# Sum of the attended values in a delta-rule decoder layer: the output halves of odd pairs are swapped and get a bank of their own

## The chip, the cores and the metric

One core of one Trainium2 chip. The time is device microseconds of one execution of the whole program, from the first to the last instruction with what the runtime counts around it; lower is better. Three runs of the kernel before gave a median of 2584.98 us (2584.34 to 2587.34).

TensorE (PE in the profile) multiplies. A product loads one operand into the array (LDWEIGHTS, engine PEld) and streams the other past it (MATMUL); the result lands in PSUM, eight banks of 128 partitions by 512 fp32. A product smaller than the array sits on a tile of it, `tile_position=(row, column)`: the rows are the partitions that the operands come from, the columns the partitions that the sum goes to. Products on different tiles can run at the same time. A product of fp32 operands is recorded as two LDWEIGHTS and two MATMULs. VectorE is DVE, ScalarE is ACT, GpSimd is POOL, and SyncE (SP) issues every DMA from one queue, in order. Engines wait for each other through semaphores.

## The reference

A decoder layer over 64 sequences of 64 tokens with 256 features: a gated delta-rule attention with 16 heads, then a cross attention, then a ternary feed-forward, each with its layer norm and its residual. Only the first part is touched. Cut to it:

```python
q = _causal_conv_silu(x @ Wq, qcw, qcb).reshape(b, t, HK, DK)
k = _causal_conv_silu(x @ Wk, kcw, kcb).reshape(b, t, HK, DK)
v = _causal_conv_silu(x @ Wv, vcw, vcb).reshape(b, t, HK, VE)
...
def step(state, inp):
    state = state * at
    err = vt - einsum('bhkv,bhk->bhv', state, kt)
    state = state + bt * einsum('bhk,bhv->bhkv', kt, err)
    return state, einsum('bhkv,bhk->bhv', state, qt)
...
out = outs.reshape(b, t, HV * DV) @ Wo
x = x + out
```

The kernel doesn't run the recurrence token by token. For each head it forms a 64x64 matrix M per sequence (the mix: how much of each earlier token's value goes to each token) and multiplies it with the values already multiplied by their part of Wo: `x + sum over heads of M_head @ (v_head @ Wo_head)`. That product with M is what the change rewrites.

## The kernel before, in words

**Tiling.** The 64 sequences are 8 groups (`G`) of 8. A group's 512 tokens are 4 pairs (`NP`, index `a`) of 128 partitions: partitions 0-63 hold one sequence of the pair (n = 0), 64-127 the other (n = 1). 8 groups by 16 heads are 128 heads, numbered through.

**The pipeline.** Each engine runs the same list of steps (`schedule`). A step has a value head `v` and a key head `k` that is 20 heads ahead; `w` is the head before `v`. 20 steps have only `k`, 108 have both, 20 have only `v`, and one more finishes the last head. The middle of the list is a hardware loop of 16 steps (`Fori`, run 6 times), with five jumps back between its rounds. Within a step, TensorE does in this order (function `step`, lines as in the profile):

1. `project(v,0)`, L1270: six 128x512 fp16 products into bank 0; it needs the `XV` tile (the group's normalized input, reloaded by DMA once a group, L355).
2. `values(w,0)`, L1284: twelve 128x256 products, into `VWB`; needs `low_values` of DVE (L1035).
3. `off_diagonal(v)`, L1305, needs two DMA loads (`ld_pv` L388, `ld_en` L377); `query_sums(k-2)`, L1312, needs the squares that POOL makes (L626); `diagonal(v)`, L1321.
4. `project(v,1)`, `values(w,1)`, `correction(v)` (L1334), `project(k,2)`.
5. `outputs(w)`, **L1348**: the mix of values, eight products M (64x64) times VW (64x256), both fp32, added up over the 16 heads of a group in the banks `AC[0]` and `AC[1]`. It needs the values as ACT has scaled them (L788) and M from DVE (L1030).
6. `grams(k-1)`, L1364, and `project(k,3)`.

ACT makes the first convolution tap (`tap`, L762), the silus (L768, L769, L776) and the scaling of the values (L788). DVE adds the other three taps of each of the four convolutions (L1020), makes M, the low parts of the values (L1035) and the decayed key products (L1043), which SP stores to memory (`spill`, L395).

**Every eighth step** a batch of heads goes through POOL, which inverts 32x32 triangles lane by lane (L587 to L621). For it SP has in its queue, behind the store of that step: `store_lanes` (three DMAs), `load_beta` (four), the loads for the next value head (`load_values`: up to eleven), and a step later `load_lanes` (four, L415). POOL's squares for `query_sums` come behind the first operations of the batch in POOL's order.

**Once a group** (every 16 steps): SP loads the group's rows of x into `XP[:,0]` (`residual` of SP, L447, in the step with v mod 16 = 2), DVE adds the two banks to it (`residual` of DVE, L1052, v mod 16 = 1), and SP stores the sum to `X1D` (`keep`, L452, same step). The first `outputs` of the next group waits for DVE's two adds. After the last group, the second part of the kernel (cross attention and feed-forward) starts by reading `X1D` back (`rows`, L538).

The present order of tiles in `outputs`: for each pair `a`, n = 0 on tile (0,0) and n = 1 on tile (64,64), into bank `AC[a // 2]`, columns `256 * (a % 2)`. Only two tiles of 64x64 are ever used.

The second part of the kernel has a product whose tiles are 32 rows by 64 columns (`scores`, L1437), eight of fp32 with 256 streamed columns each:

```python
for c in range(2):
    for n in range(2):
        for j in range(2):
            r = 2 * h + j
            ins = mm(SCB[h][j][64 * n:64 * n + 64, 256 * c:256 * c + 256], QT[...], KG[...],
                     start=True, stop=True, tile_position=(32 * r, 64 * n))
```

Its four tiles are two groups of rows times two groups of columns, and each group of rows writes a bank of its own (j).

Of the kernel before, what the change touches and what calls it, by code (L numbers as in the profile page):

```python
# [6 lines left out]
ALU = mybir.AluOpType  # L7
# [4 lines left out]
ds = bass.ds  # L12
# [3 lines left out]
E = 256  # L16
NB = 64
GT = 512
G = NB * T // GT
NP = GT // P  # L20
NH = 16
# [39 lines left out]
def build(nc, x, ctxT, ctxR, wall, wo, wab, cw, w1, b1, w2, b2, cst, out):  # L61
    ctx = ExitStack()
    with ctx:
        def sb(name, shape, dt=F32):
            return ctx.enter_context(nc.sbuf_tensor(name, shape, dt))

        def sem(name):
            return ctx.enter_context(nc.semaphore(name))
# [15 lines left out]
        XP = sb("XP", [P, 2, NP, E])  # L84
# [18 lines left out]
        M = sb("M", [P, 2, NP, T])  # L103
# [13 lines left out]
        def dram(name, shape, dt=F32):  # L117
            return nc.dram_tensor(name, shape, dt).ap()
# [10 lines left out]
        X1D = dram("X1D", [G, P, NP, E])  # L129
# [7 lines left out]
        VW = XN[:, 1]  # L137
# [49 lines left out]
        AC = BANK[6:8]  # L187
# [22 lines left out]
        S = {n: sem(n) for n in names}  # L210
# [7 lines left out]
        def at(count):  # L218

            return count + 1  # L220


        def heads(h, per=1, more=0):

            g, off = h
            return g * (NH * per) + (off * per + more + 1)
# [16 lines left out]
        def groups(h, per=1, more=0):  # L243

            g, off = h
            return g * per + ((off // NH) * per + more + 1)
# [43 lines left out]
        def _(sp):  # L290
# [12 lines left out]
            for g in range(G):  # L303
# [9 lines left out]
                if g >= 4:  # L313
                    n = g - 4
# [119 lines left out]
            def store_lanes(k):  # L434
# [5 lines left out]
                sp.dma_start(KND[b].rearrange("o p x -> (o p) x"), KNL[:, :]).then_inc(S["st_le"], 16)  # L440
                sp.dma_start(QND[b].rearrange("o p x -> (o p) x"), QNL[:, :]).then_inc(S["st_le"], 16)

            def residual(g):

                sp.wait_ge(S["st_x1"], at(g * 16))
                sp.nop(nofuse=True)
                sp.dma_start(XP[:, 0], x[ds(g, 1)].rearrange("o p n e -> (o p) n e")).then_inc(S["ld_xa"], 16)  # L447

            def keep(g):
                sp.wait_ge(S["xa_done"], at(g * 2 + 2))  # L450
                sp.nop(nofuse=True)
                sp.dma_start(X1D[ds(g, 1)].rearrange("o p n e -> (o p) n e"), XP[:, 0]).then_inc(S["st_x1"], 16)  # L452

            def stored_eq(units):
                for s in range(2):
# [9 lines left out]
            def step(v, k):  # L465
# [13 lines left out]
                if exists(v):  # L479
                    v1 = (v[0], v[1] + 1)  # L480
                    if exists(v1):
                        load_values(v1)
                        if v1[1] % NH == 0:
                            load_xv(v1)
                    if v[1] % NH == 1 and after(v, NH):
                        keep(v[0] + (v[1] // NH - 1))
                    if v[1] % NH == 2:
                        residual(v[0] + v[1] // NH)
# [39 lines left out]
            def attended(i):  # L528
                s = i % 2
                if i >= 2:  # L530
                    sp.wait_ge(S["vb_done"], at(2 * i - 2))
                for n in range(2):
                    sp.dma_start(VTS[s][64 * n:64 * n + 64], ctxR[i]).then_inc(S[f"ld_vt{s}"], 16)

            def rows(i):
                s = i % 3
                sp.wait_ge(S[f"st_out{s}"], at(16 * (i // 3)))
                sp.dma_start(XC[s], X1D[i]).then_inc(S[f"ld_y{s}"], 16)  # L538
# [5 lines left out]

            keys(0)
            keep(G - 1)
            attended(0)
            sp.wait_ge(S["st_x1"], at(16 * G))
            rows(0)
            rows(1)  # L550
            keys(1)
# [343 lines left out]
        def _(dve):  # L895
            start_counts(dve, "dve")
            V_ = nc.vector
# [148 lines left out]
            def residual(g):  # L1046

                dve.wait_ge(S["out_mm"], at(g * NH + NH))
                dve.wait_ge(S["ld_xa"], at(g * 16 + 16))
                for n in range(2):  # L1050
                    xv = XP[:, 0, 2 * n:2 * n + 2, :].rearrange("p a e -> p (a e)")
                    V_.tensor_tensor(xv, AC[n][:, :], xv, ALU.add).then_inc(S["xa_done"], 1)  # L1052

            def step(v, k):
                if exists(v):
                    if v[1] % NH == 1 and after(v, NH):
                        residual(v[0] + (v[1] // NH - 1))
# [29 lines left out]

            schedule(dve, step)
            residual(G - 1)

            def arrived(i):
# [119 lines left out]
        def _(pe):  # L1211
            start_counts(pe, "pe")
            mm = nc.tensor.matmul
# [124 lines left out]
            def outputs(w):  # L1338
                g, off = w
                pe.wait_ge(S["vw_ev"], heads(w, 2, 2))  # L1340
                pe.wait_ge(S["m_done"], heads(w, 1, 1))
                if off % NH == 0:
                    pe.wait_ge(S["xa_done"], groups(w, 2))
                pe.nop(nofuse=True)
                for a in range(NP):
                    for n in range(2):
                        b = slice(64 * n, 64 * n + 64)
                        ins = mm(AC[a // 2][b, E * (a % 2):E * (a % 2) + E], M[b, off % 2, a, :], VW[b, a, :],  # L1348
                                 start=(off % NH == 0 and a % 2 == 0), stop=(off % NH == NH - 1), tile_position=(64 * n, 64 * n), skip_group_check=True)
                ins.then_inc(S["out_mm"], 1)  # L1350

            def grams(v, k):
# [14 lines left out]
            def step(v, k):  # L1367
# [24 lines left out]
                if exists(w):  # L1392
                    outputs(w)
# [195 lines left out]
```

## Time and profile before

| | |
|---|---|
| median of three runs | 2584.98 us |
| the profiled execution: its own time | 2580.95 us |
| span in its profile | 2579.1 us |
| granted TensorE clock, mean over the span | 0.933 |
| busy: PE, DVE, ACT, POOL | 86%, 71%, 57%, 42% |
| L1348, the mix of values | 2048 records, 248.9 us busy, 7% of the chain that ended last |
| the 128 blocks of L1348 | first at 357.1 us, last record starts at 2018.0 us |

How to read it: the profile was taken of one execution, whose own time is 4.0 us below the median of the three; the span leaves 1.9 us of that time outside. Busy time of an engine counts overlapping records once. "Idle before" an operation, with an arrow, names what the engine waited for; "issue" is a wait for nothing that the profile shows.

### The profile page before, as it was taken

The numbers are of one execution on the slowest core, as the hardware profiler recorded it, in microseconds if no ns is written. First come the engines' busy times: TensorE is split into PE (matmuls) and PEld (weight loads), VectorE is DVE, ScalarE is ACT, GpSimd is POOL, SyncE is SP. The second block draws the span as 40 slices with busy tenths as digits, with TensorE's granted clock in tenths as the row PEclk, the third lists the DMA queues.
The fourth block names the chain that finished last, engine by engine and source line by source line (L and its number), as shares of the span: only waits on it lengthen the run. The fifth ranks groups of instructions, "written<-read, shape, count | busy, mean of one in ns | idle before, by whom it ended". The sixth has DMA issues, their size and how long they took to land.

```text
span 2579.1 us, 64198 instructions
## 1 busy us (share of the span) xinstructions
PE 2218.8 (86%) x22592; PEld 1422.6 (55%) x22592; DVE 1841.7 (71%) x2925; ACT 1477.5 (57%) x2755; POOL 1088.6 (42%) x1439
## 2 busy tenths in 40 slices
PE   2486689999999999999999999999888688778787
PEld 2232245656655565565555556566555466666665
DVE  7775577877878887787778878878555545655655
ACT  3475556666666666666666666666555344544544
POOL 1016484572845638356283653836620111212222
PEclk9998889999999999999999999999999658878878
DMA  7446523243242333324324233342421101100100
GB/s 292 143 116 134 132 73 83 78 97 85 71 99 79 83 90 88 87 68 92 95 68 95 88 79 84 96 89 63 97 57 39 53 13 30 30 27 29 29 14 18
DMA packets 500783, 205.23 MB, mean 80 GB/s; under 512 B 437072, under 2 KB 454224, under 8 KB 498512
## 3 DMA queue, kind: packets, MB, share of 16 engines
q1 hardware_dynamic: 500432, 200.76, 30.7%
q8 instruction: 195, 3.19, 0.5%
q14 instruction: 156, 1.28, 0.2%
HBM read 128.33 MB, written 72.35 MB: 78 GB/s over the span
## 4 chain that ended last, share of the span: by engine, by line
PE 56%; issue 13%; SPq 8%; ACT 8%; DVE 8%; DMA 4%; POOL 2%; ACTq 0%; POOLq 0%; DVEq 0%
PE PS L1270 16%; PE PS L1284 10%; PE PS L1348 7%; PE PS L1456 3%; PE PS L1437 3%; PE PS L1470 3%; PE PS L1364 3%; DVE Y L1020 3%; ACT XN L788 3%; PE PS L1321 2%; PE PS L1498 2%; ACT Y L769 2%; SPq L377 1%; DMA SCR<-PGD 1%; SPq L431 1%
## 5 line engine op out<-in xcount | busy, mean ns | idle before, releaser
L1020 DVE SCALAR_TENSOR_TENSOR Y<-PS,CW,Y 128x504 f32<-128x504 f32 (+2 forms) x1536 | 1115.3, 732 | 442.5 <-ACT Y L762 389.9
L762 ACT ACTIVATE Y<-PS,CW 128x512 f32<-128x512 f32 x512 | 398.1, 777 | 466.4 <-PE PS L1270 454.8
L1284 PE MATMUL PS<-WOS,XN 128*128 128x256 f16 x3072 | 378.2, 273 | 2.2 <-DVE XN L1035 1.1
L1284 PEld LDWEIGHTS PS<-WOS,XN 128*128 128x128 f16 x3072 | 300.9, 98 | 92.9 <-issue 2.1
L626 POOL TENSOR_TENSOR SQ<-KQ 128x512 f32<-128x512 f32 x128 | 137.6, 1075 | 461.8 <-PE PS L1312 370.3
L1270 PE MATMUL PS<-XK,WH 128*128 128x512 f16 x1024 | 312.6, 387 | 16.3 <-DMA XK<-XHD 16.3
L1270 PE MATMUL PS<-XV,WH 128*128 128x512 f16 x1024 | 307.5, 382 | 8.4 <-issue 7.8
L612 POOL TENSOR_TENSOR SCR<-SCR 128x31 f32<-128x31 f32 (+15 forms) x496 | 291.2, 587 | 38.9
L1348 PE MATMUL PS<-XN,M 64*64 64x256 f32 x2048 | 248.9, 381 | 48.9 <-ACT XN L788 48.0
L609 POOL TENSOR_TENSOR SCR<-SCR 128x31 f32<-128x31 f32 (+15 forms) x496 | 260.3, 525 | 33.0
L788 ACT ACTIVATE XN<-PS,KN 128x256 f32<-128x256 f32 x512 | 212.6, 466 | 62.6 <-PE PS L1284 62.5
L1348 PEld LDWEIGHTS PS<-XN,M 64*64 64x64 f32 x2048 | 158.3, 132 | 137.6 <-issue 101.5
L768 ACT ACTIVATE XN<-Y 128x512 f16<-128x512 f32 x256 | 160.1, 626 | 77.2 <-PE PS L1284 74.5
L1270 PE MATMUL PS<-XK,WL 128*128 128x512 f16 x512 | 197.0, 385 | 0.0
L1035 DVE TENSOR_TENSOR XN<-Y,XN 128x512 f16<-128x512 f32 x256 | 186.6, 729 | 12.0 <-ACT Y L769 12.0
L1270 PE MATMUL PS<-XV,WL 128*128 128x512 f16 x512 | 194.7, 380 | 0.0
L776 ACT ACTIVATE KQ<-Y 128x512 f32<-128x512 f32 x256 | 159.8, 625 | 41.2 <-DVE Y L1020 27.8
L865 ACT ACTIVATE WH<-PS 128x512 f32<-128x512 f32 x128 | 73.6, 596 | 176.3 <-PE PS L1456 176.3
L769 ACT ACTIVATE Y<-Y 128x512 f32<-128x512 f32 x256 | 157.5, 615 | 0.0
L692 POOL CAST WH<-WOS 128x512 f16<-128x512 f32 x64 | 40.1, 627 | 274.9 <-ACT WOS L874 273.4
L1364 PE MATMUL PS<-KQ 128*64 128x128 f32 x2048 | 140.9, 280 | 11.4 <-ACT SCR L802 10.2
L1270 PEld LDWEIGHTS PS<-XV,WH 128*128 128x128 f16 x1024 | 87.6, 98 | 112.5 <-issue 20.3
(138 smaller groups left out, 3152.3 us busy)
## 6 DMA issues: line engine op xcount, KB each, us to landing
PGD<-SCR SPq DMA_DIRECT2D x128, 256.0 KB, 2.1
SCR<-PGD SPq DMA_DIRECT2D x128, 256.0 KB, 3.1
EQD<-XN SPq DMA_DIRECT2D x32, 512.0 KB, 4.1
SCR<-EQD SPq DMA_DIRECT2D x128, 128.0 KB, 2.6
SCR<-QND SPq DMA_DIRECT2D x128, 128.0 KB, 3.3
XP<-in_x SPq DMA_DIRECT2D x16, 512.0 KB, 4.6
SCR<-in_wall SPq DMA_DIRECT2D x8, 1024.0 KB, 7.1
SCR<-PGD SPq DMA_DIRECT2D x64, 128.0 KB, 3.0
```

The costliest lines, as they stand in the source:

```text
L609: nc.gpsimd.tensor_tensor(t, LP[:, j, j + 1:BL][:, :, None].broadcast_to([P, n, m]), LY[:, j, 0:m][:, None, :].broadcast_to([P, n, m]), AL ...
L612: nc.gpsimd.tensor_tensor(LY[:, j + 1:BL, 0:m], LY[:, j + 1:BL, 0:m], t, ALU.subtract).then_inc(S["lane"], 1)
L762: A_.activation(Y[:, b, :], PJ[b][:, :], ACT.Identity, scale=CW[:, h[1] % NH, cw0 + 3:cw0 + 4], bias=CW[:, h[1] % NH, cw0 + 4:cw0 + 5]).th ...
L768: A_.activation(VHL[:, 0, b, :], Y[:, b, :], ACT.Silu)
L769: A_.activation(Y[:, b, :], Y[:, b, :], ACT.Silu).then_inc(S[f"silu{b}"], 1)
L788: ins = A_.activation(VW[:, a, :], VWB[:, E * i:E * i + E], ACT.Copy, scale=KN[:, kn, l:l + 1])
L1020: V_.scalar_tensor_tensor(yv[:, :, m:T], pv[:, :, 0:T - m], CW[:, h[1] % NH, cw0 + 3 - m:cw0 + 4 - m], yv[:, :, m:T], ALU.mult, ALU.add).t ...
L1035: V_.tensor_tensor(VHL[:, 1, b, :], Y[:, b, :], VHL[:, 0, b, :], ALU.subtract).then_inc(S["vl_done"], 1)
L1270: ins = mm(PJ[b][:, :], wt[:, c, w0:w0 + P], xb[:, xi, :], start=(n == 0), stop=(n == 5))
L1284: ins = mm(VWB[:, E * i:E * i + E], VHL[:, vk, n, P * a:P * a + P], WOS[:, wk, 2 * (w[1] % NH) + n, :], start=(t == 0), stop=(t == 5))
L1348: ins = mm(AC[a // 2][b, E * (a % 2):E * (a % 2) + E], M[b, off % 2, a, :], VW[b, a, :], start=(off % NH == 0 and a % 2 == 0), stop=(off % ...
L1364: ins = mm(gram[64 * n:64 * n + 64, a], KQ[:, s, 0, c0:c0 + 64], KQ[:, s, :, c0:c0 + 64], start=True, stop=True)
```

## The change

`outputs` gives the products of odd pairs the swapped column half: output tile (64n, 64((n + a) mod 2)). The even pairs go to bank `AC[0]` (tiles (0,0) and (64,64)), the odd pairs to `AC[1]` (tiles (0,64) and (64,0)); so the sums of odd pairs lie with the two sequences in swapped halves of the partitions. `residual` of DVE therefore adds bank n to the pairs n, n+2 (a strided view), and the rows of x are loaded and stored with the odd pairs' halves swapped: three DMAs in place of one, for the load and for the store, and the counts of `ld_xa` and `st_x1` go from 16 to 48 a group.

```diff
+            def swapped(sums, rows):
+
+                yield sums[:, 0:NP:2, :], rows[:, 0:NP:2, :]
+                yield sums[0:64, 1:NP:2, :], rows[64:128, 1:NP:2, :]
+                yield sums[64:128, 1:NP:2, :], rows[0:64, 1:NP:2, :]
+
             def residual(g):
 
-                sp.wait_ge(S["st_x1"], at(g * 16))
+                sp.wait_ge(S["st_x1"], at(g * 48))
                 sp.nop(nofuse=True)
-                sp.dma_start(XP[:, 0], x[ds(g, 1)].rearrange("o p n e -> (o p) n e")).then_inc(S["ld_xa"], 16)
+                xg = x[ds(g, 1)].rearrange("o p n e -> (o p) n e")
+                for dst, src in swapped(XP[:, 0], xg):
+                    sp.dma_start(dst, src).then_inc(S["ld_xa"], 16)
 
             def keep(g):
                 sp.wait_ge(S["xa_done"], at(g * 2 + 2))
                 sp.nop(nofuse=True)
-                sp.dma_start(X1D[ds(g, 1)].rearrange("o p n e -> (o p) n e"), XP[:, 0]).then_inc(S["st_x1"], 16)
+                x1 = X1D[ds(g, 1)].rearrange("o p n e -> (o p) n e")
+                for src, dst in swapped(XP[:, 0], x1):
+                    sp.dma_start(dst, src).then_inc(S["st_x1"], 16)
...
-            sp.wait_ge(S["st_x1"], at(16 * G))
+            sp.wait_ge(S["st_x1"], at(48 * G))
...
                 dve.wait_ge(S["out_mm"], at(g * NH + NH))
-                dve.wait_ge(S["ld_xa"], at(g * 16 + 16))
+                dve.wait_ge(S["ld_xa"], at(g * 48 + 48))
                 for n in range(2):
-                    xv = XP[:, 0, 2 * n:2 * n + 2, :].rearrange("p a e -> p (a e)")
-                    V_.tensor_tensor(xv, AC[n][:, :], xv, ALU.add).then_inc(S["xa_done"], 1)
+                    xv = XP[:, 0, n:NP:2, :]
+                    V_.tensor_tensor(xv, AC[n][:, :].rearrange("p (a e) -> p a e", e=E), xv, ALU.add).then_inc(S["xa_done"], 1)
...
-                if off % NH == 0:
+                first = off % NH == 0
+                if first:
                     pe.wait_ge(S["xa_done"], groups(w, 2))
                 pe.nop(nofuse=True)
                 for a in range(NP):
                     for n in range(2):
-                        b = slice(64 * n, 64 * n + 64)
-                        ins = mm(AC[a // 2][b, E * (a % 2):E * (a % 2) + E], M[b, off % 2, a, :], VW[b, a, :],
-                                 start=(off % NH == 0 and a % 2 == 0), stop=(off % NH == NH - 1), tile_position=(64 * n, 64 * n), skip_group_check=True)
+                        b, o = slice(64 * n, 64 * n + 64), 64 * ((n + a) % 2)
+                        ins = mm(AC[a % 2][o:o + 64, E * (a // 2):E * (a // 2) + E], M[b, off % 2, a, :], VW[b, a, :],
+                                 start=(first and a < 2), stop=(off % NH == NH - 1), tile_position=(64 * n, o), skip_group_check=True)
```

## Rows read from the trace of the kernel before

**Rows 1.** The profile page: its head, busy times, and one of its costliest groups.

```profile
span 2579.1 us, 64198 instructions
...
PE 2218.8 (86%) x22592; PEld 1422.6 (55%) x22592; DVE 1841.7 (71%) x2925; ACT 1477.5 (57%) x2755; POOL 1088.6 (42%) x1439
...
L1348 PE MATMUL PS<-XN,M 64*64 64x256 f32 x2048 | 248.9, 381 | 48.9 <-ACT XN L788 48.0
```

**Rows 2.** Two stretches: length, busy by engine, PEclk, DMA share, GB/s.

```profile
1021.58:1034.72 13.14, 12.99 (x136) 8.04 (x137) 11.12 (x18) 8.69 (x18) 6.56 (x3) 1.00 0.23 57
...
1061.00:1075.32 14.32, 13.07 (x137) 8.09 (x137) 10.76 (x17) 8.64 (x18) 2.51 (x3) 1.00 0.65 131
```

**Rows 3.** Waits of PE, 360 to 2000 us: total us, times, longest.

```profile
...
PE PS L1312 <- POOL SQ L626: 15.8, 13, 1.9
PE PS L1305 <- DMA SCR<-PGD: 12.4, 12, 1.6
PE PS L1270 <- issue: 7.8, 5, 1.7
PE PS L1305 <- issue: 2.2, 1, 2.2
```

**Rows 4.** Timeline of PE in one step: start, length, line, records, idle before.

```profile
1021.58 1.94 PE L1348 MATMUL PS<-XN,M 64*64 64x256 f32 x16 [0.15 <-ACT XN L788]
1023.45 1.09 PE L1364 MATMUL PS<-KQ 128*64 128x128 f32 x16
```

**Rows 5.** The same view in the second part: L1437, fp32, 256 columns.

```profile
2200.53 1.09 PE L1437 MATMUL PS<-SCR,KQ 32*64 32x256 f32 x16
```

**Rows 6.** Timeline of DVE in the same step as rows 4.

```profile
1025.24 0.68 DVE L1043 TENSOR_TENSOR SCR<-PS,SCR 128x512 f32<-128x512 f32 x1
1026.80 4.46 DVE L1020 SCALAR_TENSOR_TENSOR Y<-PS,CW,Y 128x504 f32<-128x504 f32 x6 [0.88 <-ACT Y L762]
```

**Rows 7.** Timeline of SP's queue, 1050 to 1084 us.

```profile
1052.26 0.36 SPq L395 DMA_DIRECT2D PGD<-SCR  x1
...
1065.68 0.36 SPq L388 DMA_DIRECT2D SCR<-PGD  x1
```

**Rows 8.** Timeline of PE over the same stretch.

```profile
1047.86 1.94 PE L1348 MATMUL PS<-XN,M 64*64 64x256 f32 x16 [0.15 <-ACT XN L788]
...
1069.08 0.44 PE L1305 MATMUL PS<-SCR 32*32 32x32 f32 x16 [1.10 <-DMA SCR<-PGD]
...
1083.57 0.43 PE L1312 MATMUL PS<-SQ,ONES 128*32 128x128 f32 x8 [0.91 <-POOL SQ L626]
```

**Rows 9.** Timeline of POOL, 1070 to 1084 us.

```profile
1072.81 0.32 POOL L587 TENSOR_SCALAR KD<-SCR 128x32 f32<-128x32 f32 x1 [16.03 <-DMA SCR<-PGD]
...
1082.38 1.04 POOL L626 TENSOR_TENSOR SQ<-KQ 128x512 f32<-128x512 f32 x1
```

**Rows 10.** Timeline of ACT in the step behind the loop's jump.

```profile
1019.56 0.63 ACT L768 ACTIVATE XN<-Y 128x512 f16<-128x512 f32 x1 [0.30 <-DVE Y L1020]
```

**Rows 11.** The XV load: SP's issue, its landing (view of L355), PE's next projection.

```profile
979.93 0.35 SPq L355 DMA_DIRECT2D XV<-XHD  x1
...
DMA to landing us min/median/max: 3.9/4.2/4.8
...
984.42 0.59 PE L1270 MATMUL PS<-XV,WH 128*128 128x512 f16 x2
```

**Rows 12.** Timeline of DVE and PE, last steps.

```profile
1904.84 1.94 PE L1348 MATMUL PS<-XN,M 64*64 64x256 f32 x16 [1.55 <-ACT XN L788]
...
1905.96 0.69 DVE L1035 TENSOR_TENSOR XN<-Y,XN 128x512 f16<-128x512 f32 x1 [0.62 <-ACT Y L769]
...
1908.02 1.47 PE L1284 MATMUL PS<-WOS,XN 128*128 128x256 f16 x12
```

**Rows 13.** Timeline of SP's queue where it stores a group's rows (L452).

```profile
1004.90 0.38 SPq L452 DMA_DIRECT2D X1D<-XP  x1
1010.91 0.34 SPq L395 DMA_DIRECT2D PGD<-SCR  x1
```

## The prediction

> **What bounds the kernel now.** I read the page first: PE is busy 86% of a span of 2579.1 us, and the block that the change rewrites has 2048 records, 16 for each of 128 heads [rows 1]. Then the busy time by stretches: in a plain step of 13.14 us PE is busy 12.99 at full clock, DVE 11.12, ACT 8.69 [rows 2]. So TensorE sets the pace, and the reader should see how near DVE is: 2.0 us of slack in 13.14. Then PE's waits [rows 3]: 13 for POOL's squares, 12 for a DMA and one more listed as issue (2.2), 5 at the loop's jumps; before the mix of values itself it waits for ACT, 0.15 us in a plain step [rows 4] and 1.55 in the last steps [rows 12]. The waits of rows 3 decide how much of a gain survives.
>
> **The price of the block.** From the start of the mix to the start of the next block PE spends 1023.45 - 1021.58 = 1.87 us, and its 16 records span 1.94 [rows 4]. One record of fp32 with 256 columns, if pairs share the array, has 1.87 / 8 = 0.23 us a pair. The block of scores has the same number of records, columns and type, on four tiles (two groups of rows by two of columns), and spans 1.09 [rows 5]. That is the shape that the change asks for, so the block should shrink by 1.94 - 1.09 = **0.85 us**. Bounds: nothing at all if the four don't overlap; not more than half of 1.87, 0.94. I take 0.85, from the nearest row. What rows 5 don't show: tiles of 64 rows instead of 32, and two groups of rows in one bank (each keeps to its own half of the partitions, as the pairs of rows 4 do today).
>
> The page TensorEngine Tiling (Array Packing) of the Trainium skill, section Gotcha 1: PSUM Pressure, says that different row tiles cannot use the same PSUM bank at the same time. Today tiles (0,0) and (64,64) are two row tiles in one bank, and they do overlap: alone, 16 records of a pair's 0.23 us would take 3.7 us, not 1.94. By that rule the change could give nothing; it is rival B.
>
> **Plain steps.** The wait before the mix (0.15) hangs on ACT, which hangs on PE's own `values` product before it; between the two lie `correction` and a projection, which don't change. So the wait stays and the 0.85 passes on to `grams` and `project(k,3)`. What is late next? DVE: it finishes L1043 at 1025.24 + 0.68 = 1025.92 and then idles 0.88 us for the tap of that projection [rows 6]. The tap comes 0.85 sooner and 0.03 of idle is left. It just fits; the squeezed step is 12.29 us with 11.12 of DVE in it. A plain step gives the full 0.85.
>
> **Steps around a POOL batch.** Here a chain runs beside PE. SP waits for DVE's L1043, stores at 1052.26, and then issues without a break (three stores, four loads of beta, six for the next values) until the load of L388 at 1065.68 [rows 7]; PE waits for that at 1069.08, 1.10 us [rows 8]. The lanes' load goes out behind it; POOL starts on it at 1072.81 and comes to the squares 9.57 us later, at 1082.38 [rows 9]; PE waits for them until 1083.57 [rows 8]. The chain starts 4.4 us behind the mix of 1047.86, after DVE work that the change doesn't touch. It is SP's, the DMA's and POOL's time from there on, so 1083.57 stays 35.7 us behind 1047.86 whatever PE saves between. Three mixes lie in it (at 1047.86, 1061.00 and 1075.32; the stretch between the latter two stands in [rows 2]). Their 0.85 turn into longer waits: 1.10 becomes 2.8, 0.91 becomes 1.8. With 13 such batches [rows 3] that takes 39 blocks. The last batch has only the first wait (the one listed as issue): 2 more. 128 - 41 = 87 blocks count: 87 x 0.85 = 74.0 us.
>
> **The loop's jumps.** Behind a jump ACT starts L768 at 1019.56 with 0.30 us of waiting for DVE, not PE [rows 10]; DVE has lost its own time to the jump. PE's next mix hangs on it, so the block before each of the five jumps gives nothing either (I take 0.8 lost of 0.85): -4.0 us.
>
> **The XV load.** SP issues it at 979.93, behind the same kind of burst; it lands 4.2 us later, at about 984.13, and PE starts on it at 984.42 [rows 11]. PE would now come at 983.57 and wait some 0.6, with the landing's spread (up to 4.8) 0.7. Of the seven loads I count five so tight: -3.5 us.
>
> **The last 20 steps.** PE idles 1.55 us a step for ACT, behind its own `values`, so the mix is still on the path. DVE's low part is done at 1905.96 + 0.69 = 1906.65 and `values` starts at 1908.02 [rows 12]: 1.37 of slack for 0.85. Full gain, already in the 87.
>
> **DMAs and DVE's adds.** Load and store of the group's rows go from 1 DMA to 3, +4 issues a group, at the store's 0.38 us and with 0.2 between two issues some 2.3 us on SP. They come in steps with v mod 16 = 1 and 2, the bursts with v mod 8 = 4 and 5. What is queued behind them is the next `spill`, which waits for DVE: behind the store, issued at 1004.90, it goes out at 1010.91, with 5.6 us of nothing between [rows 13]. That gap hides the new issues. If it were gone: 8 x 2.3 = 18 us. Only the very last store is in the open, since the second part reads it back: 2 more issues, +0.7 us (bounds: 0 and 3, should the smaller pieces land a microsecond later each). DVE's two adds keep their element count: 0; bounds -0.2 and +0.3 us a group, on DVE, whose slack takes it.
>
> **Sum:** 74.0 - 4.0 - 3.5 - 0.7 = 65.8 us less. The profiled execution took 2580.95; 2580.95 - 65.8 = 2515. The median of the three runs is 4.0 above that execution, so the forecast for it is **2519 us**, 2.5% less.
>
> **Rivals.**
> - **A2, nothing absorbed.** If the chains at the batches move along with PE, up to 128 x 0.85 = 109 us: 2476. Against it: SP's issues and POOL's 9.57 us have fixed lengths. The middle (half of the 41 blocks saved) is 2500. Chance 0.08 for anything below 2498.
> - **B, two at a time still.** A bank serves one group of rows (or the halves of a 64-row tile block each other): no gain, and the DMAs: 2585 to 2588. For it: rows 5 keep one bank to each group of rows, as if someone had to. Against it: today's pairs share a bank. Chance 0.06.
> - **C, DVE takes over.** Its idle of 0.88 is used up to 0.03. If in the plain steps the taps slip by half the gain, 0.42 x 87 = 37 us are lost: 2556. For it: DVE at 11.12 of 12.29 us, and its two adds in one step of 16. Against it: DVE has begun L1043, and so is done with the low parts, at 1025.24 [rows 6], while PE has `grams` (begun at 1023.45, rows 4) and two projections before it asks for them. Chance 0.10 for 2548 and more.
> - **E, slower.** The array must run empty at each turn between the diagonal and the crossed pairs: three turns a block. A turn costs up to one pair's time, 0.23; the point of decision is any price over zero with no overlap of the four. Half of it: 3 x 0.12 x 128 = 45 us, 2630; whole: 2675. Against it: rows 5 turn in the same way, and 1.09 leaves no room for it. Chance 0.03.
> - The change does as it says: the four tiles of one round are (0,0), (64,64), (0,64), (64,0), all different.
>
> **How the numbers follow.** My forecast's own range is 2498 to 2540 (blocks at 0.75 to 0.94, 80 to 107 of them counting, DMA terms at their ends), chance 0.73. The range is 2498 to 2550, which reaches to the near end of C and leaves out A2, B, E and the rest of C. A measurement tells about 0.2% (5 us) from no change. Faster by more: A, A2, C, 0.91; within: B, 0.05; slower: E and a bad end of B, 0.04.
>
> **What would show it.** L1348: 16 records in 1.09 us, starts in fours. Plain step 12.3 us; the last steps 0.85 shorter too. PE's waits for POOL and for `PGD` loads up from 15.8 and 12.4 to some 27 and 34; about five for `XV`. DVE's idle of 0.88 gone. I would be wrong in the price if L1348 stays at 1.94 or lands between; wrong in the bound if the block is 1.09 and the plain step isn't 12.3; wrong on the batches if their waits don't grow.

## The result, and the profile after

The changed kernel takes 2552.34 us (2548.81 to 2560.02, four runs), the kernel before 2586.16 us (2584.34 to 2588.78); ratio 0.9873, interval 0.9859 to 0.9886. It is faster by 1.3%, 34 us. The forecast was 2519, with a range up to 2550: the sign was right, the size half of what was forecast, and the time lies just outside the range.

The profile page of the changed kernel: its head, the busy times, and two of its costliest groups. The lines of the code have moved down by 10 or 11.

```profile
span 2547.2 us, 64266 instructions
...
PE 2140.5 (84%) x22592; PEld 1352.7 (53%) x22592; DVE 1854.4 (73%) x2925; ACT 1476.6 (58%) x2755; POOL 1086.6 (43%) x1439
...
L1280 PE MATMUL PS<-XV,WH 128*128 128x512 f16 x1024 | 318.9, 394 | 21.3 <-DMA XV<-XHD 10.7
...
L1359 PE MATMUL PS<-XN,M 64*64 64x256 f32 x2048 | 140.1, 387 | 51.0 <-ACT XN L798 47.9
```

TensorE's 2048 records of the mix (L1359, before L1348) now cover 140.1 us where they covered 248.9 [rows 1]: 108.8 us less. In the trace the records of a block now start in fours (0, 8, 14 and 21 ns into it, the next four from 239 ns on), where before they started in pairs (0 and 7, then 238): the four tiles do run at a time. The timeline of TensorE over a batch, the counterpart of [rows 4, 8]:

```profile
1040.91 1.09 PE L1359 MATMUL PS<-XN,M 64*64 64x256 f32 x16 [0.15 <-ACT XN L798]
1041.94 1.09 PE L1375 MATMUL PS<-KQ 128*64 128x128 f32 x16
...
1053.20 1.09 PE L1359 MATMUL PS<-XN,M 64*64 64x256 f32 x16
...
1063.01 0.64 PE L1315 MATMUL PS<-SCR 32*32 32x32 f32 x16 [3.68 <-DMA SCR<-PGD]
...
1071.77 1.09 PE L1359 MATMUL PS<-XN,M 64*64 64x256 f32 x16 [0.15 <-ACT XN L798]
...
1078.32 0.43 PE L1322 MATMUL PS<-SQ,ONES 128*32 128x128 f32 x8
...
1084.19 1.09 PE L1359 MATMUL PS<-XN,M 64*64 64x256 f32 x16
```

The block spans 1.09 us (1.94 in rows 4), and the plain step 1053.20 - 1040.91 = 12.29 us, as forecast. Then comes the load's wait: 3.68 us where it was 1.10. The forecast had 2.8 for it, so 0.9 us is lost against the forecast up to its end. More is lost behind it: from the load's release to the next mix TensorE needs 1071.77 - 1063.01 = 8.76 us; before it needed 1075.32 - 1069.08 = 6.24 for the same products (the time of the mix at 1075.32 is the end of the second stretch of [rows 2]). Why is in the view by stretches (length, busy time by engine, then PEclk, DMA share, GB/s):

```profile
1042.00:1048.00 6.00, 6.00 (x76) 3.84 (x76) 5.66 (x9) 3.61 (x8) 0.06 (x1) 1.00 0.21 69
1062.76:1066.00 3.24, 2.99 (x42) 1.95 (x43) 0.00 (x0) 0.68 (x3) 0.00 (x0) 0.50 1.14 204
1066.00:1070.00 4.00, 4.00 (x32) 2.33 (x31) 1.16 (x2) 1.07 (x3) 2.75 (x3) 0.67 0.25 74
```

Before the wait the granted clock is 1.00 (2.4 GHz); when TensorE comes out of it, it is 0.50 (1.2 GHz), and 0.67 on the mean over the next 4 us. The page TensorE: Matmul & The Clock Gate of the Trainium skill, in Part 1 (the clock gate), lists these two levels and lets idle lead to the lower; the trace agrees here, with 0.50 behind 3.68 us of idle (further down stands a wait of nearly that length that left 1.00). In the kernel before, 1.10 us of idle left the clock at 1.00. Over the whole stretch from the first mix to the last the clock records of the trace hold two stretches at half clock, 6.8 us together, before the change, and 18, 75.1 us together, after it: 12 at the batches, two behind waits for XV (the tile of the group's input), one behind a jump and three in the last 20 steps.

The other waits of TensorE in the changed kernel (total us, times, longest), to be held against [rows 3]:

```profile
PE PS L1315 <- DMA SCR<-PGD: 37.6, 14, 4.2
PE PS L1322 <- POOL SQ L636: 17.5, 11, 3.4
PE PS L1280 <- DMA XV<-XHD: 10.7, 4, 3.4
PE PS L1280 <- issue: 10.6, 5, 2.8
```

The load's waits went from 12.4 to 37.6 us (forecast: 34), the squares' from 15.8 to 17.5 (forecast: 27), and XV waits appeared: 10.7 us over 4. One of those, in three views: SP's issue, TensorE's start, and the stretch behind it (length, busy by engine, PEclk, DMA share, GB/s):

```profile
755.79 0.35 SPq L355 DMA_DIRECT2D XV<-XHD  x1
```

```profile
760.22 0.60 PE L1280 MATMUL PS<-XV,WH 128*128 128x512 f16 x2 [3.41 <-DMA XV<-XHD]
```

```profile
760.22:764.40 4.18, 4.18 (x22) 2.36 (x24) 1.58 (x3) 0.78 (x1) 3.71 (x7) 0.64 0.26 75
```

It waits 3.41 us, and the clock behind it is 0.64 again.

**Where the time went.** From the starts of the 128 mixes: a plain step fell from 13.14 to 12.29, which over the 107 steps from the first mix to the 108th would be 91.0 us. What these steps take beyond a plain one rose from 42.3 to 111.5 us, so 69.2 of the 91.0 were given back. In parts:

| excess over plain steps, us | before | after | rise | forecast |
|---|---|---|---|---|
| 13 batches, three steps each | 32.0 | 78.3 | 46.3 | 33.2 |
| steps with the XV load (6) | 0.8 | 14.7 | 13.9 | 3.5 |
| steps behind the five jumps | 8.9 | 15.9 | 7.0 | 4.0 |

The first row is 13 times the mean length of the three steps of a batch (41.88 before, 42.89 after) less three plain ones (39.42 and 36.87). The three rows make 67.2 of the 69.2. Most of the other 2 us stands in four steps that are 0.39 us longer; in each TensorE waits 0.22 us for DVE's low parts (L1045). The 20 steps from the 108th mix to the last fell from 210.9 to 200.4 us, and from the last mix on the kernel takes 564.4 us instead of 562.7.

### The profile page after: what moved, and what is told of

Its sections match the earlier page's. It is cut to its first block, busy times and chain, and to the rows that moved or that the text cites. A ratio compares the mean times of both kernels' runs of the same rounds, so it can differ in the third digit from the quotient of the medians.

```text
span 2547.2 us, 64266 instructions
## 1 busy us (share of the span) xinstructions
PE 2140.5 (84%) x22592; PEld 1352.7 (53%) x22592; DVE 1854.4 (73%) x2925; ACT 1476.6 (58%) x2755; POOL 1086.6 (43%) x1439
## 4 chain that ended last, share of the span: by engine, by line
PE 50%; issue 13%; DVE 13%; SPq 10%; ACT 8%; DMA 5%; POOL 1%; ACTq 0%; DVEq 0%; POOLq 0%
PE PS L1280 15%; PE PS L1294 9%; DVE Y L1030 5%; PE PS L1467 3%; PE PS L1448 3%; PE PS L1481 3%; PE PS L1359 3%; PE PS L1375 2%; PE PS L1509 2%; PE PS L1331 2%; ACT XN L798 2%; SPq L377 2%; DMA SCR<-PGD 2%; SPq L431 2%; ACT Y L779 2%
## 5 line engine op out<-in xcount | busy, mean ns | idle before, releaser
L1294 PE MATMUL PS<-WOS,XN 128*128 128x256 f16 x3072 | 386.9, 277 | 3.7 <-DVE XN L1045 2.7
L1294 PEld LDWEIGHTS PS<-WOS,XN 128*128 128x128 f16 x3072 | 305.4, 100 | 104.1 <-issue 9.9
L1280 PE MATMUL PS<-XV,WH 128*128 128x512 f16 x1024 | 318.9, 394 | 21.3 <-DMA XV<-XHD 10.7
L1045 DVE TENSOR_TENSOR XN<-Y,XN 128x512 f16<-128x512 f32 x256 | 199.7, 780 | 12.2 <-ACT Y L779 12.2
L1280 PE MATMUL PS<-XV,WL 128*128 128x512 f16 x512 | 201.6, 394 | 0.0
L1359 PE MATMUL PS<-XN,M 64*64 64x256 f32 x2048 | 140.1, 387 | 51.0 <-ACT XN L798 47.9
L1375 PEld LDWEIGHTS PS<-KQ 128*64 128x64 f32 x2048 | 109.8, 137 | 67.0 <-issue 45.5
```

The source lines that it names most:

```text
L1045: V_.tensor_tensor(VHL[:, 1, b, :], Y[:, b, :], VHL[:, 0, b, :], ALU.subtract).then_inc(S["vl_done"], 1)
L1280: ins = mm(PJ[b][:, :], wt[:, c, w0:w0 + P], xb[:, xi, :], start=(n == 0), stop=(n == 5))
L1294: ins = mm(VWB[:, E * i:E * i + E], VHL[:, vk, n, P * a:P * a + P], WOS[:, wk, 2 * (w[1] % NH) + n, :], start=(t == 0), stop=(t == 5))
L1359: ins = mm(AC[a % 2][o:o + 64, E * (a // 2):E * (a // 2) + E], M[b, off % 2, a, :], VW[b, a, :], start=(first and a < 2), stop=(off % NH = ...
L1375: ins = mm(gram[64 * n:64 * n + 64, a], KQ[:, s, 0, c0:c0 + 64], KQ[:, s, :, c0:c0 + 64], start=True, stop=True)
```

## The experiments

Twelve kernels ran, four at a time beside the kernel before. A median of the kernel before holds for the kernels named behind it until the next one is given.

### Fill the idle of the first wait

```diff
+                if v[1] % 8 == 6:
+                    for _ in range(12):
+                        mm(CH[:, :], IDH[:, :], MASKN[:, :, :].rearrange("p h t -> p (h t)"), start=True, stop=True)
                 pe.wait_ge(S[f"ld_pv{s}"], pairs(v, 16, 16))
```

> The changed kernel with 12 throw-away products (fp16, 512 columns, 0.216 us each at full clock, 2.6 us in all) on TensorE ahead of the wait for the L388 load, in the one step of eight where that wait is long (37.6 us over 14 waits in the changed kernel). They go to a bank that holds nothing at that moment. Theory 1 (the idle of about 3 us drops TensorE's clock to half for 3.4 to 6.8 us, and that is what was lost): the clock drops around the batches vanish (19 stretches between 340 and 1970 us in the changed kernel, most behind such a wait), the time falls by 10 to 25 us, to 2527 to 2542, although TensorE does 34 us of work more. Theory 2 (SP's queue and the DMA landings alone set the loss, the clock is a bystander): the waits shrink by what the fillers take, the time stays within 3 us of 2552 or rises.

2546.66 us (before 2583.25; ratio 0.9864, interval 0.9841 to 0.9888). The half-clock stretches behind the load's wait went, but 17 stretches, 58.0 us together, stood elsewhere: ten behind the wait for the squares, four behind the jumps, three in the last steps. The waits for the squares and for the load:

```profile
PE PS L1325 <- POOL SQ L636: 30.0, 13, 2.7
PE PS L1318 <- DMA SCR<-PGD: 2.3, 3, 1.0
```

The load's wait fell to 2.3 us, that for the squares rose from 17.5 to 30.0. So TensorE came sooner to the second wait, as its end is set by POOL, and lost its clock there in ten of the 13 batches. The three steps of a batch took 43.3 us on the mean, not less than the 42.9 of the changed kernel. Neither theory was right by itself; the ratio can't be told from 0.9873.

### Shorten the chain: seven DMAs a step earlier

```diff
-                if ph == 0 and exists(back(k, 16)):
-                    store_lanes(back(k, 16))
-                if ph == 0 and exists(back(k, 8)):
-                    load_beta(back(k, 8))
+                if ph == 7 and exists(back(k, 15)):
+                    store_lanes(back(k, 15))
+                if ph == 7 and exists(back(k, 7)):
+                    load_beta(back(k, 7))
```

In the changed kernel:

> The changed kernel, with store_lanes and load_beta (seven DMAs, some 5.2 us of SP's issue time) moved from the step where the next value head's loads wait behind them to the step before. Both theories say that the chain of SP, DMA and POOL ends 5 us sooner, so the waits for the PGD loads (37.6 us) and for POOL's squares (17.5 us) go to nearly nothing, and with them the clock drops behind them: 2586 - 128 x 0.85 - 28 (the waits of the kernel before) + 8 for jumps and XV loads = about 2457; range 2440 to 2480. If the blocks' gain were lost to something else than this chain (DVE, say), it would stay above 2500.

2503.9 us (ratio 0.9698, interval 0.9666 to 0.9729): 48 us below the changed kernel, but 47 above what I expected, and above the 2500 that I had set as the sign of another cause. In the kernel before:

> The same move of store_lanes and load_beta in the kernel before, without the change. Its waits at the batches are 28.2 us (15.8 for POOL, 12.4 for the DMA), and there are nearly no clock drops (6.8 us of half clock): so 2586 - 28 = 2558, range 2550 to 2565. Together with the run of the same move on the changed kernel it tells what the change is worth when the chain is not in its way: theory: 128 x 0.85 = 109 us less a few for the loop's jumps, 95 to 109.

2557.48 us (ratio 0.9901, interval 0.9878 to 0.9924), as expected. The waits for the squares, first of the changed kernel with the move, then of the kernel before with it, and the timeline of TensorE around one such wait in the first of them, with the stretch behind it:

```profile
PE PS L1322 <- POOL SQ L636: 33.3, 13, 3.4
```

```profile
PE PS L1312 <- POOL SQ L626: 11.2, 13, 1.1
```

```profile
410.65 1.09 PE L1359 MATMUL PS<-XN,M 64*64 64x256 f32 x16 [0.15 <-ACT XN L798]
...
419.90 0.65 PE L1322 MATMUL PS<-SQ,ONES 128*32 128x128 f32 x8 [2.76 <-POOL SQ L636]
...
427.24 1.09 PE L1359 MATMUL PS<-XN,M 64*64 64x256 f32 x16 [0.15 <-ACT XN L798]
```

```profile
420.00:423.60 3.60, 3.60 (x30) 1.82 (x31) 0.00 (x0) 0.72 (x3) 2.94 (x9) 0.55 0.57 39
```

The load's wait is gone in both. The squares' wait is not: it has 11.2 us in the kernel before, 33.3 in the changed one, over 13 each. What I had overlooked is that the chain is not one but two: the move frees the load of L388, while the lanes' load still waits for the step's store, and POOL still makes its first operations (9.57 us, rows 9) before the squares. The faster TensorE comes to that wait 3 x 0.85 us sooner; the wait grew by 1.7 us on the mean, since the squares too were ready a little sooner (34.16 us behind the batch's first mix, 34.50 in the kernel before with the move). Behind the wait shown the clock is 0.55. From the squares' release to the next mix it takes 427.24 - 419.90 = 7.34 us there; in every batch without such a stretch it is 5.87, in this kernel, in the changed one and in the kernel before alike. **A half-clock stretch with nothing behind it that waits longer costs about 1.5 us** (with one, the way from release to mix takes 7.2 to 7.6 us in all these kernels). The kernel before with the move has no such stretch from its first mix to its last.

Not every wait of this length is followed by one. The longest wait for the squares in the changed kernel with the move is 3.43 us, and the clock stays at 1.00 in it and behind it (timeline of TensorE, then the stretches of the wait and behind it):

```profile
841.37 0.43 PE L1322 MATMUL PS<-SQ,ONES 128*32 128x128 f32 x8 [3.43 <-POOL SQ L636]
```

```profile
837.90:841.38 3.48, 0.05 (x5) 0.04 (x3) 2.31 (x4) 1.07 (x3) 3.32 (x5) 1.00 0.56 28
841.38:845.00 3.62, 3.62 (x42) 2.37 (x42) 0.34 (x1) 1.50 (x4) 2.92 (x10) 1.00 0.47 51
```

Nine of the 13 waits for the squares in this kernel have a half-clock stretch behind them, four have not; what decides is not shown.

### The squares ahead of POOL's first operations

```diff
+                if ph == 2 and exists(back(k, 1)):
+                    squares(back(k, 1))
                 if exists(kb):
                     if ph == 2:
                         lanes_begin(kb)
...
-                if exists(back(k, 1)):
+                if ph != 2 and exists(back(k, 1)):
                     squares(back(k, 1))
```

With the seven DMAs moved as well. In the changed kernel, and then in the kernel before:

> The changed kernel with two moves: the seven DMAs of store_lanes and load_beta a step earlier, as before, and in POOL's batch step the squares ahead of lanes_begin instead of behind its 9.6 us. What is left of batch waits with the first move alone is 33.3 us for POOL's squares over 13 waits, and 14 half-clock stretches (48 us up to 1930 us) behind them. Theory (fixed chains and the clock behind their waits took the gain): both go, 33 us of waits and up to 24 us of clock: 2504 - 33 - 20 = 2451, range 2440 to 2465. Rival (DVE, or SP at the XV load, takes the gain): above 2480.

> The same two moves in the kernel before. With the first move alone its waits for the squares are 11.2 us and it has no half-clock stretch between 350 and 1950 us: 2557 - 11 = 2546, range 2540 to 2552. The difference to the changed kernel with both moves is what the four tiles are worth when nothing else is in their way; theory 90 to 105 us (128 x 0.85 less the loop's jumps and the split DMAs).

2485.42 us (before 2588.07; ratio 0.9595, interval 0.9565 to 0.9625) and 2553.59 us (ratio 0.9867, interval 0.984 to 0.9894). No wait for squares is left in either. The first lies in the rival's range (above 2480), not in the theory's, and the rival had named the XV load: the next chain had come up. The second is 1.6 us above its range. The difference of the two kernels is 68 us, not the 90 to 105 expected. TensorE's largest new wait in the changed kernel with both moves, and the same in the kernel before with both:

```profile
PE PS L1282 <- DMA XV<-XHD: 22.7, 7, 4.3
```

```profile
PE PS L1272 <- DMA XV<-XHD: 10.9, 6, 2.4
```

### Fill the idle, once more

Twelve products of 512 columns ahead of the load's wait and 14 of 384 columns ahead of the squares', in the changed kernel; and the 14 alone, in the changed kernel with the seven DMAs moved:

```diff
             def query_sums(k):
+                if k[1] % 8 == 1:
+                    for _ in range(14):
+                        mm(CH[:, 128:512], IDH[:, :], MASKN[:, 0:6, :].rearrange("p h t -> p (h t)"), start=True, stop=True)
                 pe.wait_ge(S["sq"], heads(k, 1, 1))
```

> The changed kernel with throw-away products ahead of both waits of a batch: 12 of 512 columns before the L388 load's, 14 of 384 columns before POOL's squares (2.3 us). The chain of SP and POOL is as in the changed kernel; only TensorE's idle is filled. With the first fill alone, 16 half-clock stretches were left (55 us, most of them behind the wait for the squares) and the time was 2547. Theory 1 (the clock takes a part of the loss): stretches fall to below 6, the time to 2547 - 16 = 2530, range 2522 to 2540. Theory 2 (the clock is a bystander, since the waits' ends are set by SP and POOL): 2545 to 2550.

> The changed kernel with the seven DMAs moved, and 14 throw-away products of 384 columns ahead of the wait for POOL's squares, which stays (33 us over 13 in the run without the fill). Theory 1: the 14 half-clock stretches (48 us) go, each worth 1.7 us: 2504 - 20 = 2484, range 2478 to 2490. Theory 2: 2500 to 2506.

2548.82 us (ratio 0.9847, interval 0.9814 to 0.9879) and 2505.46 us (ratio 0.9686, interval 0.9657 to 0.9715). The clock came back as meant: 5 stretches (23.9 us) and 3 (13.7 us) were left, and from release to mix the first kernel takes 5.87 us in all 13 batches, the second in 12 of them (7.45 in the first batch). The time did not follow: both lie in the ranges of theory 2. The fill in the second kernel:

```profile
1051.62 2.45 PE L1321 MATMUL PS<-MASKN,IDH 128*128 128x384 f16 x14
...
1055.49 0.42 PE L1325 MATMUL PS<-SQ,ONES 128*32 128x128 f32 x8 [1.42 <-POOL SQ L636]
...
1061.35 1.09 PE L1362 MATMUL PS<-XN,M 64*64 64x256 f32 x16 [0.15 <-ACT XN L798]
```

It lies within the wait (1.42 us are left), so it is not the fill itself. Two things took the gain back. The squares' release came later behind the batch's first mix: 34.67 us on the mean, 34.16 without the fill (and 37.01 with both fills, 36.53 in the changed kernel). The last of the four loads of lanes took 3.70 us to land here, 2.82 without the fill; why is open. So of the 0.9 us a batch that the clock gave back (6.90 us from release to mix became 5.99), 0.4 was left, some 5 us in all. And the steps behind the five jumps took 24.2 us over plain ones here, 26.0 in the kernel with both fills, against 13.7 to 19.3 in the seven kernels with the four tiles that have no fill or only the one ahead of the load's wait. In three of the five, TensorE waits a second time in both kernels with the 14 products (L1294, 0.7 to 1.5 us, "issue"), which happens in none of the others. More instructions stood in the loop's body. That these made the jumps dearer is my reading, not tested by itself. What the runs show is that filling the idle raises the clock and gains nothing that can be measured here, while removing the wait does.

### The XV load sooner, and the split DMAs

```diff
-                        load_values(v1)
-                        if v1[1] % NH == 0:
-                            load_xv(v1)
+                        load_values(v1, (lambda: load_xv(v1)) if v1[1] % NH == 0 else None)
```

where `load_values` now calls what it is given behind its EN loads. With the two moves before, in the changed kernel and in the kernel before:

> The changed kernel with the two moves for the batches and a third: the XV load goes to SP's queue in the middle of the next head's loads (behind the four of EN, ahead of T1 and PGV) instead of behind them all. With two moves TensorE waits 22.7 us over 7 times for XV. The load goes out some 2 us sooner, so each wait (3.2 us on the mean) shrinks to about 1.2 and the half-clock stretches behind them (10 left) mostly go: 2485 - 14 - 10 = 2461, range 2452 to 2472. If the wait is not set by SP's queue but by the projection that frees the tile, nothing changes: 2480 to 2488.

> The same three moves in the kernel before. Its waits for XV with two moves were 10.9 us over 6; they should go: 2553 - 9 = 2544, range 2538 to 2550. Against the changed kernel with the same moves it gives what the four tiles are worth with the chains out of the way: theory 128 x 0.85 = 109 less 8 for the loop's jumps and 9 for the split DMAs: 80 to 95 us.

2455.52 us (before 2583.59; ratio 0.9506, interval 0.9478 to 0.9533) and 2539.4 us (ratio 0.9832, interval 0.9806 to 0.9857). Both in their ranges. TensorE's waits behind the jumps (issue) and for XV in the first, and behind the jumps in the second, which has none for XV:

```profile
PE PS L1282 <- issue: 11.5, 5, 2.5
PE PS L1282 <- DMA XV<-XHD: 3.1, 6, 0.9
```

```profile
PE PS L1272 <- issue: 7.9, 5, 1.8
```

The difference of the two kernels is the worth of the change with these chains out of the way: 2539.4 - 2455.5 = 84 us, against 34 with them (54 with the first move in both, 68 with two).

The split DMAs were looked at from both ends: alone in the kernel before, and taken out of the changed kernel (the sequences of odd pairs swapped on the host, so that load and store are one DMA again and the second part works on swapped pairs), without and with the three moves.

```diff
-                for dst, src in swapped(XP[:, 0], xg):
-                    sp.dma_start(dst, src).then_inc(S["ld_xa"], 16)
+                sp.dma_start(XP[:, 0], xs[ds(g, 1)].rearrange("o p n e -> (o p) n e")).then_inc(S["ld_xa"], 16)
...
+    xs = a["x"][perm].reshape(G, NP, P, E).transpose(0, 2, 1, 3)
+    c = a["ctx_512"][perm]
```

> The kernel before with only the DMAs of the change: load and store of a group's rows in three pieces each, halves not swapped, two tiles as before. In the changed kernel the way from the last add to the second part's first LayerNorm product grew: TensorE waits 14.98 us there against 13.09. Theory: 1.5 to 2.5 us slower than before, all of it at the end of the first part, the group's loads and stores in the loop cost nothing. Rival: the splits also disturb the loop (more packets, SP later at the XV load): 5 us and more.

> The change as it is, only without the split DMAs (sequences of odd pairs swapped on the host instead). If the 9.6 us that the split cost the kernel before are a cost of the change too: 2552 - 9 = 2543, range 2539 to 2547. If it is hidden behind the longer waits of the changed kernel apart from the end of the first part: 2549 to 2552.

> The changed kernel with the three moves and without the split DMAs: the sequences of odd pairs are swapped on the host (a second, permuted copy of x for the residual, permuted context, permuted rows of the result), so load and store of a group's rows are one DMA each again and the second part works on swapped pairs. The split alone cost the kernel before 9.6 us (2592.8 against 2583.3). Theory: 5 to 10 us less than with the three moves and the split: about 2454, range 2445 to 2462.

Alone in the kernel before: 2592.81 us against 2583.25 (ratio 1.0037, interval 1.0023 to 1.0052), so 9.6 us slower and not 2. Of that, 1.7 us stand at the end of the first part; the waits for its first norm and for the squares are

```profile
PE PS L1426 <- DVE XN L1116: 14.8, 1, 14.8
PE PS L1322 <- POOL SQ L636: 19.8, 13, 2.6
```

(13.1 us in the kernel before; the squares' wait was 15.8.) In its profile four batches have a half-clock stretch behind the squares, where the kernel before has one, and their way from release to mix is 7.5 us. The two profiled executions lie 15.6 us apart: the three steps of a batch took 42.54 us on the mean, 41.88 before, which is 8.6 us over the 13, and from the last mix on it is 568.8 us against 562.7. Taken out of the changed kernel, the split gives nothing: 2552.35 us (before 2583.59; ratio 0.9871, interval 0.9839 to 0.9903). In that kernel's profile the batches took 8.5 us less and the steps with the XV load 12.5 more than in the changed one: what one chain gave, the other took. Taken out where the waits are gone, the kernel takes 2449.64 us (ratio 0.9485, interval 0.946 to 0.951) against 2455.52; the intervals of the two ratios overlap, so the 6 us are likely but not shown. That kernel is the best of the study, 5.2% below the kernel before.

## Why the prediction was wrong

The step that failed is the price of the waits around TensorE. The prediction let a wait grow by the blocks saved, 33.2 us at the batches and 3.5 at the XV loads, and put what stands behind it at nothing. Measured were 46.3 and 13.9 us: the clock behind the waits, a chain that itself ended later, and XV waits that grew beyond the saved block.

**The price of the block held.** 1.09 us as in rows 5, 0.85 saved, in all 128 heads. Rivals B and E are out: two row tiles in one bank, each on its own half of the partitions, and crossed with two others in a second bank, overlap at the rate of the scores' block. The rule of the Trainium skill on row tiles and banks (TensorEngine Tiling (Array Packing), Gotcha 1: PSUM Pressure) does not hold in the form quoted in the prediction: both traces are against it. Two row tiles that write the same partitions of one bank were not tried.

**Plain steps held**, 12.29 us to the hundredth; so did the last ones (9.62 for 10.47). Rival C is out: DVE kept up, but for the four steps of 0.39 us more. It idles 0.20 us before the tap of `project(k,3)`, where 0.03 was left by my sum:

```profile
1045.28 4.45 DVE L1030 SCALAR_TENSOR_TENSOR Y<-PS,CW,Y 128x504 f32<-128x504 f32 x6 [0.20 <-ACT Y L772]
```

**Steps around a batch: the mechanism was right, a term was missing.** "1083.57 stays 35.7 us behind 1047.86 whatever PE saves between": over the 13 batches the squares' release stood 35.88 us on the mean behind the batch's first mix before, and 36.53 after. Three savings a batch were absorbed, as forecast, and the runs with shortened chains show that it is this chain (34 us of gain with it, 84 without it and the XV chain). Two things came on top. The chain itself grew by 0.65 us. On the mean it didn't grow up to the load of L388, whose release stood 21.08 us behind the first mix before and 21.09 after, but behind it: the last of the four loads of lanes landed 0.42 us later (25.37 for 24.95), POOL's first operations took 9.70 us for 9.57, and in the first batch TensorE itself came 0.8 us late to the squares, at half clock. Single batches also lose ahead of L388: in the one above, four EN loads took 4.43 us (SP's timeline, issue to issue):

```profile
1045.31 0.36 SPq L395 DMA_DIRECT2D PGD<-SCR  x1
...
1053.01 4.43 SPq L377 DMA_DIRECT2D SCR<-ED  x4
...
1059.53 0.36 SPq L388 DMA_DIRECT2D SCR<-PGD  x1
...
1061.55 2.96 SPq L415 DMA_DIRECT2D SCR<-PGD  x4
```

From the first to the L388 load it is 14.22 us, where rows 7 have 13.42. What slows the issues and the landings wasn't found. And a wait of TensorE was booked at its length alone. It has a second price, the clock behind it. Behind the first wait of a batch the second wait mostly hides that (in 8 of the 12 batches with such a stretch the way from release to mix was the plain 5.87 us); behind the second it does not. Together 1.0 us a batch (0.65 the chain, 0.4 the clock behind the second wait), 13 us.

**The XV load: mis-sized, 13.9 instead of 3.5 us.** I left SP's issue where it was and let TensorE come 0.85 us sooner. But the issue hangs on the batch's third mix, through DVE's L1053 and the store (in the profile after, at 745.00, 4.5 us behind the mix of 740.54, and XV goes out at 755.79). That mix is made late by the half clock, the next one is not, since the squares' wait had room; so the delay that the squares' wait hides comes back as a wait for XV, 3.41 us in the case shown, with a half-clock stretch behind it. The other loads bear this out: the four that TensorE waits for come after batches with a half-clock stretch behind the first wait (7.8 to 8.9 us from the load's release to the mix), the two that it doesn't wait for after batches without one there (6.23 us). The four waits make 10.7 us; two of them have such a stretch behind them, which is most of the rest.

**The jumps: 7.0 instead of 4.0 us.** TensorE's wait behind them grew from 7.8 to 10.6 us, and one of the five steps (4.5 us over a plain one, the others 2.5 to 3.1) has a half-clock stretch. The cost of the five spreads from kernel to kernel by more than 3 us (13.7 to 19.3 us), so I would not read more into it.

**The last steps and the end: 10.6 us less instead of 15.3 (18 blocks), and 1.7 more instead of 0.15 less.** Two of the last steps now have a half-clock stretch (11.3 us instead of 9.6), though TensorE's 1.55 us of idle in them is the same as before; only the block in front of it is shorter. The step before the last mix kept its length (6.86 for 6.87), since TensorE now waits 0.77 us in it for DVE's low parts. And the last store in three pieces cost 1.9 us more before the second part (14.98 us of waiting for its first norm, 13.1 before), not 0.7: the pieces took 1.94 us to issue.

Added up, against the forecast: 13 (batches) + 10.4 (XV) + 3.0 (jumps) + 4.7 (last steps) + 1.9 (end), less 1.3 us by which the first mix came sooner, and some 2 us in other steps: 34 us, which is what lies between 2515 and the profiled execution's 2548.81.

The range was too narrow because it left no room for dearer chains: every term of the batches and of the XV load was priced at its mean length of waiting, though three chains beside TensorE were at the edge at once, and only DVE (rival C) was given a bad end.

## What to carry to other kernels

When TensorE gets faster in a kernel where it is the bound, look for every chain beside it that starts from one of its products and ends in one of its waits, and count how many of the saved pieces lie between start and end: where TensorE already waits for the chain, each of them is lost. Then shorten the chains before judging the change: here three small moves of issues and of one POOL operation made it worth 84 us instead of 34. A wait of TensorE behind which the granted clock shows 0.50 is dearer than its length, by about 1.5 us here, unless a later wait has room to hide it.

## What the runs showed of the hardware that I had not expected

- The clock: 1.10 us of idle in the plain course of a batch left 1.00, 3.68 us gave 0.50. But waits went either way at nearly every length: of the kernel before's 13 waits for the squares, one of 1.75 us has a half-clock stretch behind it and the longest, 1.87 us, has none; with only the DMAs of a group split it is four of 13 (1.46 to 2.58 us), while others of 1.62 to 1.74 us have none; and with the seven DMAs moved a wait of 3.43 us has none. So the length of a wait alone does not tell the two apart; in two of the last steps the wait stayed at 1.55 us, and only the block in front of it got shorter.
- Throw-away products ahead of both waits of a batch kept the clock at 1.00 behind them (5.87 us from release to mix in all 13 batches), and still gained nothing.
- Splitting two DMAs of 512 KB a group into three pieces each cost 9.6 us where 2 were expected, though SP had idle time there; in the profile 8.6 us stand in the batches and only 1.7 in the wait at the end of the part, where it would be seen at once.
- Crossed 64-row tiles of fp32 with running sums cost exactly what 32-row tiles with fresh sums cost: 1.09 us for 16 records.
